# Ten of sixteen heads convolved in fp32, their diagonals wrapped by four heads, in a one-core decoder kernel

## The reference

```python
x = x + attention(layernorm(x))                     # 16 heads of 16 channels
# cross term: ctx is both k and v, in 32 groups of 8 channels
kv = einsum('bhil,bhjl->bijhl', k_, v_)             # products of two channels of a group
y  = irfft(rfft(kv, n=2L) * rfft(ssm_kernel, n=2L))[..., :L]   # causal convolution over L = 256
out = y + kv * D
x = x + einsum('bijhl,bhil->bjhl', out, q_)         # q = layernorm(x)
x = x + ffn(layernorm(x))                           # gelu(gate) * up, then down, weights from 4-bit codes
```

## Time and profile before

| What | Before |
|---|---|
| Median of 3 runs | 250.36 us (250.22 to 252.26) |
| Profiled execution, its time | 251.04 us |
| Its span in the trace | 249.3 us |
| PE busy | 228.1 us, 91% |
| DVE busy | 163.0 us, 65% |
| POOL busy | 147.4 us, 59% |
| ACT busy | 133.7 us, 54% |
| Clock that PE was granted | full (2.4 GHz), in all 40 slices |

### The profile page before, as it was taken

The page is one execution under the profiler, slowest core; times in us unless marked ns, Lnnn a source line. Parts: engine busy times, 40 slices in busy tenths (PEclk is TensorE's granted clock), DMA queues, the critical chain, the costliest instruction groups (busy, mean ns, idle before and its releaser), DMA issues.

```text
span 249.3 us, 5605 instructions
## 1 busy us (share of the span) xinstructions
PE 228.1 (91%) x2148; PEld 144.3 (58%) x2148; DVE 163.0 (65%) x290; ACT 133.7 (54%) x289; POOL 147.4 (59%) x174
## 2 busy tenths in 40 slices
PE   7799997997796979986999999999999999999992
PEld 7574774554463546653447586565665656556562
DVE  3889899996969899996769964236262362412134
ACT  2447898897584689655854443253152531523320
POOL 4169898592428999978997613461735617323130
PEclk9999999999999999999999999999999999999999
DMA  6985999367132102200120000021030000000005
GB/s 174 339 236 157 170 231 307 82 145 176 47 126 76 59 4 77 56 3 0 48 78 4 0 0 3 0 71 58 0 129 3 0 0 3 0 0 0 3 1 168
DMA packets 15059, 18.90 MB, mean 76 GB/s; under 512 B 1368, under 2 KB 12728, under 8 KB 15032
## 3 DMA queue, kind: packets, MB, share of 16 engines
q1 hardware_dynamic: 15032, 18.53, 26.8%
HBM read 15.23 MB, written 3.17 MB: 74 GB/s over the span
## 4 chain that ended last, share of the span: by engine, by line
PE 64%; DVE 10%; POOL 6%; ACT 5%; DMA 5%; issue 4%; SPq 4%; DVEq 0%; ACTq 0%
PE bank L1357 37%; PE bank L1538 16%; DMA X<-in_x 3%; POOL arena L482 3%; DVE mx L1047 2%; DMA XN<-in_down_scale 2%; DVE kvp L1022 2%; PE bank L1609 2%; DVE arena L1029 2%; POOL arena L485 2%; SPq L317 1%; POOL w L498 1%; PE bank L1607 1%; ACT PT L671 1%; ACT arena L637 1%
## 5 line engine op out<-in xcount | busy, mean ns | idle before, releaser
L506 POOL TENSOR_TENSOR QK<-QK 128x512 f16<-128x512 f32 x24 | 27.8, 1158 | 56.4 <-ACT QK L700 56.4
L1123 DVE SCALAR_TENSOR_TENSOR QK<-bank,QK 128x512 f32<-128x512 f32 x32 | 22.0, 689 | 59.0 <-PE bank L1357 59.0
L710 ACT ACTIVATE QK<-bank 128x512 f32<-128x512 f32 x32 | 18.9, 595 | 59.7 <-PE bank L1357 59.4
L1357 PE MATMUL bank<-xTh,Wa 128*128 128x512 f16 x128 | 40.5, 379 | 0.7 <-DVE xTl L1148 0.7
L1357 PE MATMUL bank<-xTh,Wb 128*128 128x512 f16 x128 | 40.5, 379 | 0.0
L482 POOL TENSOR_TENSOR arena<-Ys,qx 128x640 f32<-128x640 f32 x16 | 27.4, 1715 | 5.9 <-ACT qx L753 5.7
L1357 PE MATMUL bank<-xTl,Wb 128*128 128x512 f16 x64 | 24.3, 379 | 0.0
L1357 PE MATMUL bank<-xTl,Wa 128*128 128x512 f16 x64 | 24.3, 379 | 0.0
L1538 PE MATMUL bank<-Wa,QK 128*128 128x256 f16 x192 | 23.4, 273 | 0.0
L1538 PE MATMUL bank<-Wb,QK 128*128 128x256 f16 x192 | 23.3, 273 | 0.0
L1538 PEld LDWEIGHTS bank<-Wa,QK 128*128 128x128 f16 x192 | 18.8, 98 | 4.7
(11 more groups left out here) (132 smaller groups left out, 472.6 us busy)
## 6 DMA issues: line engine op xcount, KB each, us to landing
arena<-in_codes SPq DMA_DIRECT2D x6, 384.0 KB
arena<-kscr SPq DMA_DIRECT2D x2, 1024.0 KB, 7.7
QK<-qk_scratch SPq DMA_DIRECT2D x8, 256.0 KB, 5.0
arena<-in_ctx SPq DMA_DIRECT2D x2, 768.0 KB, 6.9
qk_scratch<-Wa SPq DMA_DIRECT2D x12, 128.0 KB, 3.6
arena<-in_gu_scale SPq DMA_DIRECT2D x6, 256.0 KB
QK<-qk_scratch SPq DMA_DIRECT2D x8, 128.0 KB, 5.1
out<-XN SPq DMA_DIRECT2D x4, 256.0 KB, 2.4
```

Of the source, the lines that this page charges most:

```text
L506: g_.tensor_tensor(il[:, u % IR], val[:, u % VR], ih[:, u % IR], ALU.subtract).then_inc(s_il, 1)
L710: s_.activation(val[:, u % VR], bank[2 * (u % 2)][:, :], ACT.Gelu_apprx_tanh, scale=1.0 / W_GAIN).then_inc(s_gel, 1)
L1123: v_.scalar_tensor_tensor(out=val[:, u % VR], in0=bank[2 * (u % 2) + 1][:, :], scalar=UP_SCALE, in1=val[:, u % VR], op0=ALU.mult, op1=ALU. ...
L1357: ins = mmul(out, a(c), w(c), start=(n == 0), stop=(n == 3 * len(chunks) - 1))
```

## The change

- The first ten heads (`WIDE` = 10) are convolved in fp32: `products` writes their fp32 products into `arena`, a ring of four heads in the place of the fp16 one (`KV32`), and PE multiplies them with the fp32 taps (`T32`). Such a head needs no `kv_hi` and no `kv_lo`, and has one matmul for lc = 0 and two for lc = 1. From the fifth head on `products` waits until `convolve` has read the ring's slot. The last six heads are done as before.
- Every convolution takes the 36 first of 40 columns of a batch, 288 in all. The last four are those that stand twice.
- The small copy behind each `conv_out` goes. After every fourth head ACT runs `wrap_round`: one copy for the four columns left out (64 x 4 elements) and one for the repeats behind diagonals 1 to 3 (64 x 3 x 3 elements). `conv_products` waits for the eight of these.
- The taps are stored by two DMAs, ten heads in fp32 and six as halves.
- The last two batches of the output are stored singly, batch 6 by SP and batch 7 by ACT.
- The matmuls that only keep PE busy at the start write to two banks in turn.
- The lists of all engines otherwise keep their order.

```diff
-                sp.dma_start(kscr, taps16[:, :, :]).then_inc(s_kscr, 16)
+                sp.dma_start(kscr[WIDE:H], taps16[WIDE:H, :, :].rearrange("h l s -> h (l s)").bitcast(F32)).then_inc(s_kscr, 16)
+                sp.dma_start(kscr[0:WIDE], taps[0:WIDE, :]).then_inc(s_kscr, 16)
...
-            for b in range(0, B, 2):
-                sp.wait_ge(s_fin, b + 2)
-                sp.dma_start(out_d[b:b + 2].rearrange("b t d -> t b d"), XN[:, b:b + 2, :]).then_inc(s_out, 16)
+            for b, n in ((0, 2), (2, 2), (4, 2), (6, 1)):
+                sp.wait_ge(s_fin, b + n)
+                sp.dma_start(out_d[b:b + n].rearrange("b t d -> t b d"), XN[:, b:b + n, :]).then_inc(s_out, 16)
...
                 s_.activation(view(Ys[:, h, lc], [[YROW, B], [DIAG, NPAIR], [1, HD]]),
                               conv_bank(h, lc)[:, 0:320].rearrange("p (b d m) -> p b d m", b=B, d=NPAIR),
                               ACT.Copy).then_inc(s_ys[lc], 1)
-                s_.activation(view(Ys[:, h, lc], [[YROW, B], [DIAG, 3], [1, 3]], HD),
-                              view(conv_bank(h, lc)[:, 0:320], [[40, B], [HD, 3], [1, 3]], HD + 5),
-                              ACT.Copy).then_inc(s_ys[lc], 1)
+            def wrap_round(g):
+
+                for lc in range(2):
+                    sc.wait_ge(s_ys[lc], 4 * g + 4)
+                rows = Ys[:, 4 * g, 0]
+                every = [YROW, 4 * 2 * B]
+                s_.activation(view(rows, [every, [1, 4]], 4 * DIAG + 4), view(rows, [every, [1, 4]], 4 * DIAG),
+                              ACT.Copy).then_inc(s_wrap, 1)
+                s_.activation(view(rows, [every, [DIAG, 3], [1, 3]], HD),
+                              view(rows, [every, [DIAG, 3], [1, 3]], DIAG + 5), ACT.Copy).then_inc(s_wrap, 1)
...
             act_hi(UNITS - 1)
+            sc.wait_ge(s_fin, B)
+            sc.dma_start(out_d[B - 1], XN[:, B - 1, :]).then_inc(s_out, 16)
...
-                if h >= KPR:
-                    ve.wait_ge(s_kvl[0], h - KPR + 1)
+                if h >= KPR + WIDE:
+                    ve.wait_ge(s_kvl[0], h - KPR - WIDE + 1)
+                elif KVR <= h < WIDE:
+                    for lc in range(2):
+                        ve.wait_ge(s_y[lc], h - KVR + 1)
...
+                if h < WIDE:
+                    pe.wait_ge(s_kv[0], h + 1)
+                    if lc == 0:
+                        mmul(out, T32[:, h, 0:P], wide(0), start=True, stop=True).then_inc(s_y[0], 1)
+                    else:
+                        mmul(out, T32[:, h, P:2 * P], wide(0), start=True, stop=False)
+                        pe.wait_ge(s_kv[1], h + 1)
+                        mmul(out, T32[:, h, 0:P], wide(1), start=False, stop=True).then_inc(s_y[1], 1)
+                    return
```

More of the change, by code:

```diff
@@ L21 @@
 NPAIR = 5
+NUNIQ = 36
+WIDE = 10
 NSLOT = 8
@@ L227, in lo_done, with prod @@
             return (s_ilv, u + 1) if u < 2 * EARLY - 1 else (s_il, u - 2 * EARLY + 2)
+        def prod(h, m):
+            return KV32[:, h % KVR, m, :] if h < WIDE else kvp[:, h % KPR, m, :]
         def conv_bank(h, lc):
@@ L778, in _ @@
             v_out(0)
-            kv_hi(0)
             q_hi(0, 3)
             q_hi(1, 0)
-            kv_hi(1)
             q_hi(1, 1)
-            kv_hi(2)
             v_out(1)
@@ L788, in _ @@
             v_out(2)
-            kv_hi(3)
             v_out(3)
@@ L792, in _ @@
             conv_out(0, 0)
-            kv_hi(4)
             conv_out(0, 1)
             conv_out(1, 0)
-            kv_hi(5)
             conv_out(1, 1)
             conv_out(2, 0)
-            kv_hi(6)
             v_out(5)
             conv_out(2, 1)
-            kv_hi(7)
             conv_out(3, 0)
             conv_out(3, 1)
+            wrap_round(0)
             conv_out(4, 0)
-            kv_hi(8)
             conv_out(4, 1)
@@ L811, in _ @@
             conv_out(5, 1)
-            kv_hi(9)
             conv_out(6, 0)
@@ L817, in _ @@
             conv_out(7, 1)
+            wrap_round(1)
             max_hi(0)
@@ L830, in _ @@
             conv_out(11, 1)
+            wrap_round(2)
             kv_hi(13)
@@ L848, in _ @@
             conv_out(15, 1)
+            wrap_round(3)
             probs(1, 1)
@@ L1184, in _ @@
             q_lo(0, 2)
-            kv_lo(0)
             products(1)
@@ L1334, in keep_busy @@
             def keep_busy(n):
-                for _ in range(n):
-                    mmul(bank[7][:, 0:P], ident[:, :], ident[:, :], start=True, stop=True)
+                for i in range(n):
+                    mmul(bank[6 + i % 2][:, 256:256 + P], ident[:, :], ident[:, :], start=True, stop=True)
             def transpose_x(pr):
@@ L1408, in convolve, with kv @@
                 if h >= CONV_EARLY:
-                    take(6 + lc, s_ys[lc], 2 * h + 2)
+                    take(6 + lc, s_ys[lc], h + 1)
                 elif h >= 2:
-                    pe.wait_ge(s_ys[lc], 2 * (h - 1))
-                out = conv_bank(h, lc)[:, 0:320]
+                    pe.wait_ge(s_ys[lc], h - 1)
+                out = view(conv_bank(h, lc)[:, 0:320], [[40, B], [1, NUNIQ]])
+                def kv(m, r):
+                    return view(KV[:, h % KVR, m, r, :], [[40, B], [1, NUNIQ]])
@@ new lines, in wide @@
+                def wide(m):
+                    return view(prod(h, m), [[40, B], [1, NUNIQ]])
+                if lc == 0 and h % 8 == 0:
+                    pe.wait_ge(s_toep[h // 8], 16)
+                if h < WIDE:
[7 more added lines that the diff above has]
+                    return
@@ L1413, in convolve @@
+                pe.wait_ge(s_kvl[0], h - WIDE + 1)
                 if lc == 0:
-                    if h % 8 == 0:
-                        pe.wait_ge(s_toep[h // 8], 16)
-                    pe.wait_ge(s_kvl[0], h + 1)
                     for n, (s, r) in enumerate(((0, 0), (1, 0), (0, 1))):
-                        last = mmul(out, T[:, h, 0:P, s], KV[:, h % KVR, 0, r, :], start=(n == 0), stop=(n == 2))
+                        last = mmul(out, T[:, h, 0:P, s], kv(0, r), start=(n == 0), stop=(n == 2))
@@ L1425, in convolve @@
                     for n, (s, r) in enumerate(((0, 0), (1, 0), (0, 1))):
-                        last = mmul(out, T[:, h, 0:P, s], KV[:, h % KVR, 1, r, :], start=False, stop=(n == 2))
+                        last = mmul(out, T[:, h, 0:P, s], kv(1, r), start=False, stop=(n == 2))
                     last.then_inc(s_y[1], 1)
```

57 lines of the change are left out of this document (21 added, 36 removed).

## The result

The changed kernel takes 255.36 us (median of 4, 253.53 to 257.23); before took 251.31 us (median of 4) beside it. The ratio is 1.017, 95% interval 1.010 to 1.024. So it is slower by 1.7%, outside my range. The profiled execution has 255.8 us, span 254.1 us, against 251.04 and 249.3.

What follows compares the result with a forecast made beforehand. It took `take_max(1)` to time the middle stage through SP's queue, with PE waiting at `row_scores(4, 0)`. From a median of 250.36 us, +1.4 for that delay and -0.3 for the last store gave 251.5 us, range 249.4 to 253.4.

Steps and rivals of the forecast that it cites:

- PE in the first ten heads: PE's convolution: an fp32 head takes 1.48 us, +0.25 us each, so `row_scores(0, 0)` starts at about 37.9 us.
- How much of this 1.5 us is left: From the first scores to head 11: lateness partly paid back, PE 0.5 us later at head 11's end.
- ACT and the wraps: ACT ahead of `take_max(1)`: wrap pair 0.9 us plus 0.15 waiting; with PE's 0.5, `take_max(1)` comes 1.4 us later.
- SP and `row_scores(4, 0)`: SP's queue passes on the delay of `take_max(1)`; `row_scores(4, 0)` moves from 59.64 to 61.0 us.
- Beyond 64 us ... the 1.4 us pass on: Single steps up to `gate_and_up(0)`: no list changes, so it moves by 1.4 us, from 117.69 to 119.1.
- The end: Last output store, now 128 KB on ACT instead of 256 KB: saves 0.3 us.
- rival 1: PE's fp32 matmuls each pay 0.1 us more for weights not hidden: 253.8 us, chance 0.2.
- Rivals 2 and 3: Relief wins, `take_max(1)` earlier, 249.4 us, chance 0.15; delay half absorbed between 62 and 75 us, 250.8 us, chance 0.2.
- Sum: Whole kernel: +1.4 and -0.3 us give a median of 251.5 us, slower by 0.4%.

Runs made afterwards that it cites:

- e3: Changed kernel with all 40 columns convolved, the small copies back and no wraps, ten heads still fp32; ratio 1.012 to the kernel before.
- e1: Changed kernel with the wraps moved to later places where ACT stood idle, off the way of `take_max(1)`; median 256.75 us.
- e11: Kernel before with 36 columns and the wraps by four heads at late places, no fp32 head; 250.28 us at full clock, before 250.46.
- e12: Changed kernel with four fp32 heads, late wraps and four useless matmuls ahead of `row_scores(0, 0)`; ratio 1.010 to the kernel before.
- e6: Changed kernel with late wraps and useless PE matmuls at four thin stretches; median 254.16 us, ratio 1.008 to the kernel before.
- e8: Changed kernel with the last four batches stored as before, two DMAs of two batches by SP; span 254.4 us against 254.1.
- e5: Kernel before with twelve useless fp32 matmuls at four places where PE was thin; median 250.78 us, ratio 1.001 to the kernel before.
- e9: Changed kernel with four fp32 heads, late wraps and useless PE matmuls at four thin stretches; median 250.62 us, ratio 0.999 to the kernel before.
- e7: Changed kernel with only four fp32 heads and late wraps; median 254.39 us, 249.67 to 250.09 at full clock.
- e10: Changed kernel, wraps in place, with useless PE matmuls at four thin stretches; ratio 1.011 to the kernel before, 252.85 to 254.34 us at full clock.
- e4: Changed kernel with six useless fp32 matmuls ahead of `row_scores(4, 0)`; median 253.71 us.

## Why the prediction was wrong

Its reading of what bounds the stage was right, and every checkpoint moved the way it said. Two steps failed: the sum ahead of `take_max(1)`, which let most of PE's lateness be paid back, and the clock, which it took as given.

- **"PE in the first ten heads"**: the price of a head was right (1.46 us, predicted 1.48), and so was `row_scores(0, 0)` (37.81, predicted 37.9). The step fails behind it, in "How much of this 1.5 us is left": predicted 0.5 us at the end of head 11 on PE, measured 1.3. I had let the removed `kv_lo` pay part of the lateness back. But the diff's own new wait puts `products(9)` ahead of the first maximum, released only when PE is done with head 5 and slowed by POOL's half: the first maximum came at 38.95 where I had 38.6, the second at 40.79 (40.5). DVE's time from the `kv_lo` turned into idle time ahead of the products (1.07 us each time). `row_scores(1, 0)` came 1.39 us later and its maximum 1.27, where I had 0.85: each first fp32 matmul behind scores adds 0.11 us, and two of them lie ahead. Behind it I had PE gain 0.35 us more; it gained 0.1, for two more such matmuls (0.2 us) and a wait of 0.18 us for ACT at 47.59, where I had none. That fp32 makes this lateness is shown by e3 and by e1 beside e11. That lateness passes on whole is shown by e12, though in a kernel that keeps the `kv_lo` of heads 4 to 9. How it splits between the new wait and the first matmuls is read from the traces only; a kernel with a longer ring, without the wait, would show it, and none was run.
- **"ACT and the wraps"**: 1.03 us for the pair and 0.2 of waiting, predicted 0.9 and 0.15. Moving them gives 1.1 us (e1). Slightly small, right in kind. Together with the first step: `take_max(1)` +2.37, predicted +1.4.
- **SP and `row_scores(4, 0)`**: it passed on what came (+2.55 after +2.37), as predicted. In all 13 profiles beside before's, `row_scores(4, 0)` moves with `take_max(1)` to within about 0.5 us.
- **"Beyond 64 us ... the 1.4 us pass on"**: at full clock they do, roughly: e1's +1.48 became +1.87, e6's +1.32 became +1.24. In the profiled execution of the changed kernel +2.55 became +4.76. For the 2.2 us more the prediction had no term; the trace shows two falls of the clock and one collision of DVE with POOL in that stretch. The longer idle time ahead of `row_scores(4, 0)` (2.36 us for 1.44) may favour the first fall, but this isn't shown: e8's profile has the same idle time and no fall behind it, and 17 of 23 executions of the kernel before had a mean clock of 0.993 or less on one chip. That PE's thin stretches bring falls is shown by the fillers, four places at once (e5 beside before, e9 beside e7); which place counts isn't isolated. The row on PE's clock, "full (2.4 GHz), in all 40 slices", was true of one execution and I took it as true of the kernel.
- **The end**: -0.3 us predicted, 0.0 measured (e8). By the rule of the Trainium skill that I had weighed against it ("DMA: Bandwidth & Descriptors", "Issuing engines are not separate DMA queues") the end would give nothing, and that is what came.
- **Rivals**: rival 1 came nearest with 253.8 us, close to the 252.9 and 253.5 us at full clock and 1.6 us under the measured median. Its mechanism is not what the traces show: an fp32 matmul takes 0.485 us, not 0.1 more, except the first behind scores. Rivals 2 and 3 found no support in the changed kernel. The rule of the Trainium skill on ACT ("ScalarE: Activation LUTs", "Rules for kernel authors") is given there for a bias that is a pointer operand, which these copies don't have; it would give 1.3 us for the pair by my estimate from its figures, measured 1.03.
- **Sum**: of about 4 us between the medians, 2.3 to 3.0 are there at full clock. At `take_max(1)` fp32 has the larger part of it and the wraps the smaller. The rest fits the falls of the clock, but isn't isolated: executions of before have falls too, and e6 spreads by over 3 us at a mean clock of 0.997 and more. Nor does a run split the 2.2 us after 62 us between the falls and the collision.

## What to carry to other kernels

A relief of engines that aren't waited for was worth nothing here, and lateness given to PE ahead of a string of single steps came back whole, or more (0.98 us as 1.32, e12): look for what the moved work meets on the next engine, above all for a new wait that stands ahead of the first instruction on the chain. Where a kernel has stretches in which PE is thinly used, look at the granted clock over many executions before reading a difference of 1%, and try a few matmuls of no use there; they helped the kernel before and the one with four fp32 heads clearly, the changed kernel less (e6, e10). Fuse copies by what stands behind them in the list, not by their number.

## What the runs showed of the hardware

- The clock of PE halved for some microseconds behind a stretch with PE partly idle, in some profiles and not in others, and not always at the same stretch (62 us in the changed kernel's profile, 82 us in e4's, 96 us in e3's). In the changed kernel `project_out`, L1624, took 1.71 us on the chain at half clock, where it takes 0.88 at full. Twelve fp32 matmuls at four places raised the mean clock of the kernel before from 0.990 (29 executions) to 0.997 (12).
- A two-input instruction of DVE that began just behind one of POOL (37.99 us behind 37.96) took 1.04 us for 0.48. One that began just ahead (45.65 us, POOL's at 45.69) took its 0.49, and POOL's took 1.09 for 0.80. A 0.23 us `ms` stretched to 1.64 us when it began with a 1.59 us product of POOL. In every profile with a fall of the clock between 78 and 90 us (the changed kernel, e4, e7, e8, e10, e11) the `ms` that starts between 88 and 97 us took 1.43 to 1.70 us; in the others, e3 and e12 with falls elsewhere among them, it took 0.23. That the fall shifts the engines into the collision fits this and isn't tested by itself. The Trainium skill ("SBUF — State Buffer", "SBUF: two separate sides") describes a pair of ports that DVE and POOL share and that the one which starts first holds for its whole instruction; these rows agree with it.
- The last store took 2.5 us to land with 128 KB from ACT and 2.4 us with 256 KB from SP (e8).
- An fp32 matmul of 288 columns took 0.485 us from start to start and one of 320 columns 0.54; the first one behind scores took 0.60.
